# Attention over an adjacency matrix: groups of 4, 8, 8, 8, 4 row tiles instead of 4, 6, 8, 8, 6, and a rearranged start

## The chip, the cores and the metric

The kernel runs on one core of a Trainium2 chip. The metric is the device time of one launch in microseconds (us), of which three runs are given, and the profile is of one execution of its own. The core's engines are TensorE (PE, with its weight loads shown apart as PEld), VectorE (DVE), ScalarE (ACT), GpSimd (POOL) and SyncE (SP). Each works through its own instructions in the order in which they are written, and waits on semaphores for the others. Matrix products and transposes of TensorE land in PSUM, which here is divided into two double buffers for turned pairs, and one bank each for acc0, acc1, hist and misc.

## The reference, cut to what matters

```python
Wh, We = x @ W, entity_embs @ W                 # x, entity_embs: (4096, 64)
scores = (Wh @ a1)[:, None] + (We @ a2)[None, :]
e = where(scores > 0, scores, 0.2 * scores)     # leaky ReLU
e = where(adj > 0, e, -9e15)                    # adj: (4096, 4096) int32, 0 or 1
h = softmax(e, axis=1) @ entity_embs + x
out = layernorm(x + elu(h))
```

A score is p[i] + q[j], with one number p per row and one number q per entity, so the 4096 x 4096 matrix of scores is never made by a product. What is made for each of its places is a weight, the exponential of the masked score.

## The kernel before, in words

The 4096 rows are 32 tiles of 128. They are worked on in five groups of SIZES = (4, 6, 8, 8, 6) tiles. Within a group, the 4096 entities are 32 blocks of 128, and the work on one block of one group is a step; there are 160 steps. Two blocks make a pair, so a group has 16 pairs (GROUP_PAIRS), and the program has 80. Most instructions are issued once per step or per pair whatever the group's size; the size sets how wide they are: 512, 768 or 1024 columns for 4, 6 or 8 tiles.

What happens to a pair, in order:

- **Load.** POOL issues the adjacency as chunks of four blocks, which is two pairs (load(n), lines 282 to 292), converted to bf16 on the way. The ring raw holds RAWS = 5 chunks. Chunk n waits until the pairs of chunk n - 5 have been turned. Chunks 0 to 7 belong to group 0, 8 to 15 to group 1, 16 to 23 to group 2. Chunk 7 comes in two halves.
- **Turn.** TensorE transposes the pair into one of two PSUM buffers (turn_pair, L754). Pair j needs the mask of pair j - 2 made, since that frees its buffer.
- **Mask.** ACT (L340) or DVE (L553) writes it to SBUF, scaled. The function by_dve says which engine has which pair.
- **Histogram.** TensorE multiplies the mask with codes (add_hist, L770). After a group's 16 pairs the histogram is copied by ACT (copy_hist), spread by TensorE (spread_hist, L785), and decoded by DVE (decode, L518 to L537) into one bound per row, which keeps the exponentials in range. TensorE and ACT or DVE make a row of it (make_row, L792; take_row, L541 or L370).
- **Weigh.** For every pair DVE takes the minimum of mask and bound (masked, L564), and for every step it makes the exponent (exponents, L572), ACT takes the exponential (weights, L354), and TensorE multiplies it into acc0 (features, L805) and acc1 (sums, L808). The call is weigh(g, b); five buffers hold weights.
- **Finish.** While the next group is weighed, DVE, ACT and POOL finish the group in 11 parts placed at fixed steps (FINISH_AT): division, residual, elu, layer norm. The last group is finished by itself after its last step (finish_last).

Pairs are turned ahead of the steps that weigh them: 16 pairs before step 0, then all 16 pairs of group 1 during steps 0 to 19, and after that one pair for every two steps, 44 blocks ahead. So group 1 is turned while group 0 is weighed; group 2 is turned in steps 20 to 51, group 3 in steps 52 to 83, group 4 in steps 84 to 115, and the last 44 steps turn nothing.

The start, before step 0, has chains of its own. DVE makes q for all entities (q_columns). The highest and lowest q go through TensorE and back (q_highest L713, q_to_all L717, with DVE's q_scale in between); from them DVE makes the offsets from which ACT makes codes (L388). DVE then makes p (p_columns), its highest value goes through TensorE twice (p_highest, p_to_all), and find_shift makes the shift of the exponentials. The eight rows of p, spread over all partitions, are made by TensorE (p_row, L727) in the bank misc, and are copied by ACT (L328). DVE sums the entities (L679), 65 columns in one instruction, ahead of its first mask. All engines go through the 16 pairs of group 0 with these pieces written between the pairs.

Of the kernel before, what the change touches and what calls it, by code (L numbers as in the profile page):

```python
# [7 lines left out]
SIZES = (4, 6, 8, 8, 6)  # L8
# [44 lines left out]
ROWS_FROM = 8  # L53


def attention_layernorm(nc, x, adj, ent_blocks, turned_in, weights_in, out):
# [19 lines left out]
    with ctx:  # L76
# [173 lines left out]
        def by_dve(j):  # L250

            g, k = divmod(j, GROUP_PAIRS)
            return g == 0 and k >= 7 and k % 2 == 1 or g == 1 and k % 2 == 1 or g == 2 and k in (1, 4, 8, 12)
# [68 lines left out]
        def _(act):  # L322
# [3 lines left out]
            def p_row(c):  # L326
                act.wait_ge(p_mm, c + 1)
                act.activation(pb[:, 512 * c:512 * c + 512], misc[:, :], ACT.Copy, scale=1 - ALPHA).then_inc(p_rows, 1)  # L328
# [56 lines left out]
            for j in range(4):  # L385
                store_pair(j)
            act.wait_ge(offs_done, 2)
            act.activation(codes[:, :, :], offs, ACT.Exp, bias=code_bias[:, :], scale=SPAN * LN2).then_inc(codes_done, 1)  # L388
            for j in range(4, GROUP_PAIRS):
                if j >= ROWS_FROM:  # L390
                    p_row(j - ROWS_FROM)
                store_pair(j)
            copy_hist(0)
            act.wait_ge(bias_done, 1)
# [20 lines left out]
        def _(dve):  # L415
# [256 lines left out]

            q_columns()
# [5 lines left out]
            dve.tensor_reduce(ent_part[:, :], ent_sb[:, :, :].rearrange("p b f -> p f b"), AX.X, ALU.add).then_inc(part_done, 1)  # L679
            for j in range(GROUP_PAIRS):  # L680
                store_pair(j)
            decode(0)
            take_row(0)
            dve.wait_ge(p_rows, ROWS)
            masked(0)
            dve.wait_ge(sum_mm, 1)
            dve.tensor_copy(ent_sum[:, :], misc[:, 0:FA]).then_inc(sum_done, 1)
            for g in range(NG):
                for b in range(NB):
# [7 lines left out]
                    exponents(g, b)  # L697
                    if b % 2 == 0 and s + 2 < STEPS:
# [4 lines left out]
        def _(pe):  # L703
# [15 lines left out]
            def p_row(c):  # L719

                pe.wait_ge(pcol_step, 2)
                if c == 0:
                    pe.wait_ge(shift_step, 2)
                if c:
                    pe.wait_ge(p_rows, c)
                for t in range(4):
                    ins = pe.transpose(misc[:, P * t:P * t + P], pcol[:, 4 * c + t:4 * c + t + 1].to_broadcast([P, P]), identf[:, :])  # L727
# [10 lines left out]
            def entity_sums():  # L738
                pe.wait_ge(part_done, 1)
# [34 lines left out]
            def spread_hist(g):  # L774
                pe.wait_ge(hist_copied, g + 1)
                pe.wait_ge(stack_done, 2)
                if g == 0:
                    pe.wait_ge(shift_step, 3)
                    pe.wait_ge(p_rows, ROWS)
# [15 lines left out]
            def weigh(g, b):  # L795
                i = NB * g + b
                pe.wait_ge(w_done, i + 1)
                if b == 0 and g:
# [39 lines left out]
            q_highest()  # L838
            q_to_all()
# [69 lines left out]
```

## Time and profile before

| | us |
|---|---|
| median of 3 runs | 348.91 (348.24 to 349.12) |
| the profiled execution | 347.55 |
| its span | 345.5 |
| start, to the first exponent (step 0) | 48.8 |
| group 0 weighed, to step 32 | 48.8 to 94.4 |
| group 1 | 94.4 to 151.6 |
| group 2 | 151.6 to 216.5 |
| group 3 | 216.5 to 281.3 |
| group 4 | 281.3 to 330.9 |
| the last group's finish and output | 330.9 to 345.5 |

The borders are the starts of the first exponent (L572) of each group, and the end of the last one, in the timeline of DVE. In the rows below, a window row gives the window, its length, then for PE, PEld, DVE, ACT and POOL the busy time and the count of instructions, then TensorE's granted clock as a share of 2.4 GHz, the DMA engines' share and the GB/s that they wrote. A timeline row gives start, duration (or the time from the first start to the last end where several are merged), engine, line, operation, what is written from what, the count, and in brackets the idle time before it and what ended it.

Over the whole span the page has PE busy 295.0 us (85%), DVE 306.7 us (89%) and ACT 259.3 us (75%).

### The profile page before, as it was taken

The page shows a single profiled execution, that of the slowest core. Times are in us where ns is not written, and L with a number is a line of the kernel's source. Part 1 is how long each engine was busy: PE and PEld are TensorE (multiplying, and loading weights), DVE is VectorE, ACT ScalarE, POOL GpSimd, SP SyncE. Part 2 cuts the span into 40 slices and gives each one's busy share as a digit, 9 for nine tenths or more (in the row PEclk, how much of TensorE's full clock was granted, in tenths as well). Part 3 has the DMA queues.
Part 4 walks back from the last instruction along what each step waited for, and adds up shares of the span by engine and source line. Part 5 has one row for each costly group of instructions (what it writes and reads, how often), then busy time and mean ns, then how long its engine had stood idle before and what let it go on. Part 6 is the DMA issues. An engine that isn't in the chain of part 4 may idle for free.

```text
span 345.5 us, 9074 instructions
## 1 busy us (share of the span) xinstructions
PE 295.0 (85%) x3920; PEld 160.2 (46%) x3920; DVE 306.7 (89%) x428; ACT 259.3 (75%) x262; POOL 46.4 (13%) x55
## 2 busy tenths in 40 slices
PE   1285969999999999999999999999988598876860
PEld 1154756767755555654544445445443234422320
DVE  1797169899998998889999999999999999999965
ACT  1083729787998989999999998999886567565630
POOL 6031212222121111120000002100000400000301
PEclk9998969999999999999999999999999789999995
DMA  7999999999999999799667775700000000000000
GB/s 157 255 206 201 157 189 152 185 207 208 207 207 207 196 173 159 123 143 150 95 99 111 111 109 83 125 3 2 2 0 2 2 30 3 2 1 2 0 32 24
DMA packets 35768, 37.32 MB, mean 108 GB/s; under 512 B 848, under 2 KB 34960, under 8 KB 35728
## 3 DMA queue, kind: packets, MB, share of 16 engines
q0 software_dynamic: 33936, 33.56, 61.7%
q1 hardware_dynamic: 1792, 3.18, 3.2%
q8 instruction: 31, 0.51, 0.6%
q14 instruction: 9, 0.07, 0.1%
HBM read 69.24 MB, written 1.05 MB: 203 GB/s over the span
## 4 chain that ended last, share of the span: by engine, by line
PE 43%; DVE 23%; issue 22%; ACT 7%; DMA 2%; POOL 1%; POOLq 0%; DVEq 0%; SPq 0%; ACTq 0%
PE acc L805 15%; PE pairs L754 14%; DVE xm L564 10%; PE acc L808 8%; DVE wts L572 5%; ACT mask L340 4%; PE hist L770 3%; DMA ent_sb<-ent_blocks_dram 2%; ACT wts L354 2%; DVE y L606 1%; DVE ent_part L679 1%; POOL rstd L297 1%; PE misc L727 1%; PE misc L785 1%; DVE wts L431 1%
## 5 line engine op out<-in xcount | busy, mean ns | idle before, releaser
L354 ACT ACTIVATE wts<-wts,q_bias 128x768 f32<-128x768 f32 (+2 forms) x160 | 151.2, 977 | 41.1 <-DVE wts L572 40.8
L572 DVE SCALAR_TENSOR_TENSOR wts<-pb,q_bend,xm 128x768 f32<-128x768 f32 (+2 forms) x160 | 166.3, 1063 | 2.5 <-PE acc L808 2.2
L805 PE MATMUL acc<-wts,ent_sb 128*32 128x384 f32 (+2 forms) x1280 | 151.2, 520 | 10.8 <-ACT wts L354 8.5
L340 ACT ACTIVATE mask<-pairs 128x2048 bf16<-128x2048 bf16 (+2 forms) x64 | 98.9, 1548 | 23.3 <-PE pairs L754 22.5
L808 PE MATMUL acc<-wts,onesf 128*32 128x256 f32 (+1 forms) x1152 | 91.8, 359 | 0.0
L564 DVE TENSOR_TENSOR xm<-mask,drow 128x1536 bf16<-128x1536 bf16 (+2 forms) x80 | 80.2, 1003 | 0.1
L754 PE MATMUL pairs<-ident,raw 128*128 128x128 bf16 x1024 | 75.4, 228 | 4.3 <-DVE mask L553 3.2
L754 PEld LDWEIGHTS pairs<-ident,raw 128*128 128x128 bf16 x1024 | 62.5, 102 | 26.4 <-issue 26.1
L808 PEld LDWEIGHTS acc<-wts,onesf 128*32 128x32 f32 x1152 | 40.8, 111 | 71.2 <-issue 65.5
L288 POOL DMA_DIRECT2D raw<-adj_dram x40 | 33.3, 834 | 179.0 <-PE pairs L754 178.2
L805 PEld LDWEIGHTS acc<-wts,ent_sb 128*32 128x32 f32 x1280 | 36.7, 109 | 36.6 <-ACT wts L354 17.7
L770 PE MATMUL hist<-mask,codes 128*32 128x384 bf16 (+2 forms) x320 | 33.3, 349 | 2.4 <-ACT mask L340 1.4
L297 POOL TENSOR_TENSOR rstd<-var,mhalf 128x6 f32<-128x6 f32 (+2 forms) x5 | 11.0, 2205 | 116.6 <-DVE var L643 116.6
L553 DVE TENSOR_SCALAR mask<-pairs 128x1536 bf16<-128x1536 bf16 (+3 forms) x17 | 15.7, 925 | 11.8 <-PE pairs L754 11.7
L770 PEld LDWEIGHTS hist<-mask,codes 128*32 128x32 bf16 x320 | 9.9, 96 | 9.6 <-ACT mask L340 2.2
L328 ACT ACTIVATE pb<-misc 128x512 f32<-128x512 f32 x8 | 4.8, 598 | 8.0 <-PE misc L727 8.0
L713 PE MATMUL misc<-identf,qm 128*2 128x128 f32 x2 | 0.6, 398 | 9.8 <-DVE qm L439 9.8
L792 PE MATMUL misc<-ident,dcol 128*128 128x128 bf16 x32 | 3.2, 248 | 5.5 <-DVE dcol L536 5.5
L606 DVE SCALAR_TENSOR_TENSOR y<-ent_sum,empty,misc 128x64 f32<-128x64 f32 x32 | 6.6, 273 | 0.0
L727 PE MATMUL misc<-identf,pcol 128*128 128x128 f32 x32 | 5.5, 298 | 0.9 <-DVE shift L500 0.2
L647 DVE TENSOR_TENSOR y<-y,rstd 128x384 f32<-128x384 f32 (+2 forms) x5 | 2.9, 581 | 3.8 <-POOL rstd L297 3.6
L431 DVE TENSOR_TENSOR wts<-ent_sb,wa_row 128x2048 f32<-128x2048 f32 x1 | 2.3, 2293 | 4.2 <-DMA ent_sb<-ent_blocks_dram 4.2
(107 smaller groups left out, 103.0 us busy)
## 6 DMA issues: line engine op xcount, KB each, us to landing
raw<-adj_dram POOLq DMA_DIRECT2D x16, 1024.0 KB, 12.6
raw<-adj_dram POOLq DMA_DIRECT2D x16, 768.0 KB, 8.0
raw<-adj_dram POOLq DMA_DIRECT2D x7, 512.0 KB, 12.1
ent_sb<-ent_blocks_dram SPq DMA_DIRECT2D x1, 1024.0 KB, 7.8
x_sb<-x_dram SPq DMA_DIRECT2D x2, 256.0 KB, 8.1
raw<-adj_dram POOLq DMA_DIRECT2D x2, 256.0 KB, 5.7
out_dram<-y SPq DMA_DIRECT2D x2, 256.0 KB, 2.0
x_sb<-x_dram SPq DMA_DIRECT2D x2, 192.0 KB, 8.0
```

Of the source, the lines that this page charges most:

```text
L288: pool.dma_start(raw[:, n % RAWS, 0:SIZES[g], 0:P * first], rows(adj, g)[:, :, P * CHUNK * c:P * (CHUNK * c + first)]).then_inc(adj_in[n % ...
L297: pool.tensor_tensor(rstd[:, 0:n], var[:, 0:n], mhalf[:, 0:n], ALU.pow).then_inc(rstd_done, 1)
L340: act.activation(mask[:, i % RING:i % RING + k, 0:n], pairs[j % 2][:, 0:k, 0:n], ACT.Relu, scale=2.0 ** LIFT).then_inc(act_mask_done, 1)
L354: act.activation(part, part, ACT.Exp, bias=q_bias[:, b:b + 1]).then_inc(w_done, 1)
L553: dve.tensor_scalar(mask[:, i % RING + k:i % RING + 2, 0:n], pairs[j % 2][:, k:2, 0:n], 2.0 ** LIFT, 0.0, ALU.mult, ALU.max).then_inc(dve_ ...
L564: dve.tensor_tensor(xm[:, i % XS:i % XS + 2, 0:n], mask[:, i % RING:i % RING + 2, 0:n], drow[:, g % 2, 0:n].unsqueeze(1).to_broadcast([P, ...
L572: dve.scalar_tensor_tensor(wts[:, i % SLOTS, 0:n], pb[:, P * TILE0[g]:P * TILE0[g] + n], q_bend[:, b:b + 1], xm[:, i % XS, 0:n], ALU.max, ...
L606: ins = dve.scalar_tensor_tensor(y[:, t, :], ent_sum[:, 0:F], empty[:, row:row + 1], misc[:, features_at(g, t)], ALU.mult, ALU.add)
L754: ins = pe.transpose(pairs[j % 2][:, k, P * t:P * t + P], raw[:, n % RAWS, t, at:at + P], ident[:, :])
L770: ins = pe.matmul(hist[to:to + Q, 0:n], codes[:, i % NB, :], mask[:, i % RING, n * c:n * c + n], start=(pair == 0), stop=(pair == GROUP_PA ...
L805: pe.matmul(acc[0][to:to + Q, 0:n], ent_sb[:, b, Q * f:Q * f + Q], part[:, n * k:n * k + n], start=(b == 0), stop=(b == NB - 1))
L808: ins = pe.matmul(acc[1][Q * k:Q * k + Q, 0:P * m], onesf[:, 0:Q], part[:, P * t:P * t + P * m], start=(b == 0), stop=(b == NB - 1))
```

## The change

The diff has five parts. SIZES becomes (4, 8, 8, 8, 4). TensorE turns pairs 0 to 3 before it does q_highest and q_to_all, and ACT makes codes before pair 7 and not before pair 4; the histogram's products start at pair 10, in threes. Rows of p are made in acc0 and acc1 in turn instead of misc; row 0 goes between pairs 13 and 14, the others come after the last pair. DVE's sum of the entities is cut in two halves of 32 and 33 columns, behind its masks of pairs 13 and 15, and of group 0 DVE makes these masks alone (before: pairs 7, 9, 11, 13 and half of 15). The sums of the entities are copied at step 2 and no more ahead of step 0.

```diff
-SIZES = (4, 6, 8, 8, 6)
+SIZES = (4, 8, 8, 8, 4)
...
-            return g == 0 and k >= 7 and k % 2 == 1 or g == 1 and k % 2 == 1 or g == 2 and k in (1, 4, 8, 12)
+            return g == 0 and k in (13, 15) or g == 1 and k % 2 == 1 or g == 2 and k in (1, 4, 8, 12)
...
-            for j in range(4):
-                store_pair(j)
-            act.wait_ge(offs_done, 2)
-            act.activation(codes[:, :, :], offs, ACT.Exp, bias=code_bias[:, :], scale=SPAN * LN2).then_inc(codes_done, 1)
-            for j in range(4, GROUP_PAIRS):
-                if j >= ROWS_FROM:
-                    p_row(j - ROWS_FROM)
-                store_pair(j)
+            for j in range(GROUP_PAIRS):
+                store_pair(j)
+                if j == CODES_AT:
+                    act.wait_ge(offs_done, 2)
+                    act.activation(codes[:, :, :], offs, ACT.Exp, bias=code_bias[:, :], scale=SPAN * LN2).then_inc(codes_done, 1)
+                if j == GROUP_PAIRS - 2:
+                    p_row(0)
             copy_hist(0)
+            for c in range(1, ROWS):
+                p_row(c)
...
-            dve.tensor_reduce(ent_part[:, :], ent_sb[:, :, :].rearrange("p b f -> p f b"), AX.X, ALU.add).then_inc(part_done, 1)
             for j in range(GROUP_PAIRS):
                 store_pair(j)
+                if by_dve(j):
+                    entity_part(j // (GROUP_PAIRS - 1))
             decode(0)
             take_row(0)
-            dve.wait_ge(p_rows, ROWS)
             masked(0)
-            dve.wait_ge(sum_mm, 1)
-            dve.tensor_copy(ent_sum[:, :], misc[:, 0:FA]).then_inc(sum_done, 1)
+            dve.wait_ge(p_rows, 1)
...
+                    if s == 2:
+                        dve.wait_ge(p_rows, ROWS)
+                        dve.wait_ge(sum_mm, 1)
+                        dve.tensor_copy(ent_sum[:, :], misc[:, 0:FA]).then_inc(sum_done, 1)
...
             def weigh(g, b):
                 i = NB * g + b
                 pe.wait_ge(w_done, i + 1)
+                if i == 0:
+                    pe.wait_ge(p_rows, ROWS)
...
-            q_highest()
-            q_to_all()
-            pe.wait_ge(ident_done, 4)
...
+            pe.wait_ge(ident_done, 4)
             for j in range(GROUP_PAIRS):
-                if j >= ROWS_FROM:
-                    p_row(j - ROWS_FROM)
                 turn_pair(j)
-                if j == 6:
+                if j == 3:
+                    q_highest()
+                    q_to_all()
+                if j == 12:
                     p_highest()
-                if j == 7:
+                if j == 13:
                     p_to_all()
-                if j >= 4:
-                    hist_to(j - 1)
+                    p_row(0)
+                hist_to(min(j - 1, 3 * (j - 9)))
             hist_to(GROUP_PAIRS)
+            p_row(1)
             spread_hist(0)
+            for c in range(2, 5):
+                p_row(c)
             make_row(0)
+            for c in range(5, ROWS):
+                p_row(c)
             entity_sums()
```

CODES_AT is 7, tested after store_pair(7): codes are made behind the mask of pair 7. On TensorE the program began like this before (misc<-identf,qm is the exchange's first product, pairs<-ident,raw are turns, eight per pair of group 0, hist<-mask,codes the histogram):

```order
L707 MATMUL acc<-w_sb,wts 128x64 x2
L713 MATMUL misc<-identf,qm 2x128
L717 MATMUL misc<-q_diag,onesf 128x2
L754 MATMUL pairs<-ident,raw 128x128 x40
L770 MATMUL hist<-mask,codes 32x256 x12
L754 MATMUL pairs<-ident,raw 128x128 x8
L770 MATMUL hist<-mask,codes 32x256 x4
```

Now it begins like this, still on TensorE:

```order
L716 MATMUL acc<-w_sb,wts 128x64 x2
L761 MATMUL pairs<-ident,raw 128x128 x32
L722 MATMUL misc<-identf,qm 2x128
L726 MATMUL misc<-q_diag,onesf 128x2
L761 MATMUL pairs<-ident,raw 128x128 x56
L777 MATMUL hist<-mask,codes 32x256 x12
L761 MATMUL pairs<-ident,raw 128x128 x8
```

The 32 turns of pairs 0 to 3 moved ahead of the exchange, and eleven pairs are turned before the first product with codes instead of five.

Where TensorE passes from the start to the first steps, the program before has these rows (misc<-stack spreads the histogram, misc<-ident,dcol is make_row, misc<-ent_part the sums of the entities, acc<-wts the first weigh):

```order
L770 MATMUL hist<-mask,codes 32x256 x12
L785 MATMUL misc<-stack,acc_sb 128x64 x2
L792 MATMUL misc<-ident,dcol 128x128 x4
L741 MATMUL misc<-ent_part,onesf 128x65
L754 MATMUL pairs<-ident,raw 128x128 x24
L805 MATMUL acc<-wts,ent_sb 32x256 x4
```

After the change TensorE has these in the same place (acc<-identf,pcol are rows of p, four transposes each):

```order
L734 MATMUL acc<-identf,pcol 128x128 x4
L791 MATMUL misc<-stack,acc_sb 128x64 x2
L734 MATMUL acc<-identf,pcol 128x128 x12
L798 MATMUL misc<-ident,dcol 128x128 x4
L734 MATMUL acc<-identf,pcol 128x128 x12
L748 MATMUL misc<-ent_part,onesf 128x65
L761 MATMUL pairs<-ident,raw 128x128 x32
L813 MATMUL acc<-wts,ent_sb 32x256 x4
```

Seven rows of p moved from between the pairs to around the decoding, and the first two pairs of group 1 have 32 transposes instead of 24.

## Rows read from the trace of the kernel before

**Rows 1.** Busy time of each engine by window, one per stage (columns above)
```profile
48.80:94.40 45.60, 45.17 (x832) 31.91 (x830) 42.74 (x66) 37.69 (x44) 8.60 (x10) 0.96 1.20 192
76.20:94.40 18.20, 18.20 (x351) 13.02 (x350) 16.93 (x29) 15.61 (x18) 2.64 (x3) 1.00 1.24 208
94.40:151.60 57.20, 56.69 (x793) 32.40 (x790) 52.50 (x74) 53.75 (x52) 8.05 (x9) 1.00 1.08 175
151.60:216.50 64.90, 64.83 (x851) 32.83 (x849) 63.82 (x74) 62.99 (x55) 8.35 (x9) 1.00 0.73 112
216.50:281.30 64.80, 58.56 (x704) 25.80 (x706) 64.59 (x76) 52.86 (x50) 4.63 (x2) 0.95 0.11 20
281.30:330.90 49.60, 40.42 (x476) 16.03 (x468) 49.53 (x67) 31.65 (x36) 3.21 (x1) 1.00 0.02 7
330.90:345.50 14.60, 3.35 (x35) 1.69 (x35) 7.21 (x20) 2.00 (x4) 1.32 (x1) 0.68 0.04 14
```

**Rows 2.** Timeline of TensorE in the start
```profile
14.44 0.59 PE L713 MATMUL misc<-identf,qm 128*2 128x128 f32 x2 [9.77 <-DVE qm L439]
...
32.66 1.01 PE L754 MATMUL pairs<-ident,raw 128*128 128x128 bf16 x8 [3.22 <-DVE mask L553]
...
48.40 1.91 PE L754 MATMUL pairs<-ident,raw 128*128 128x128 bf16 x16
```

**Rows 3.** Timeline of DVE in the start
```profile
28.06 3.85 DVE L679 TENSOR_REDUCE ent_part<-ent_sb 128x65 f32<-128x2080 f32 x1
```

**Rows 4.** DMA issues from 3 to 4 us: chunk 1, size, us to landing
```profile
raw<-adj_dram POOLq DMA_DIRECT2D x1, 512.0 KB, 12.1
```

**Rows 5.** Timeline of POOL: chunks 1 to 4 are issued
```profile
3.55 2.98 POOL L288 DMA_DIRECT2D raw<-adj_dram  x4
```

**Rows 6.** The tile mask, 10 to 50 us: count, duration ns min/median/max, first and last start
```profile
L340 ACT ACTIVATE mask<-pairs x12: 597/1018/1025, 17.2 to 42.9; 128x1024 bf16<-128x1024 bf16 x11, 128x512 bf16<-128x512 bf16 x1
```

**Rows 7.** Timeline of TensorE in groups 0 (turning 6 tiles) and 1 (turning 8)
```profile
62.06 0.84 PE L754 MATMUL pairs<-ident,raw 128*128 128x128 bf16 x12
62.83 0.35 PE L770 MATMUL hist<-mask,codes 128*32 128x384 bf16 x4
...
118.75 1.07 PE L754 MATMUL pairs<-ident,raw 128*128 128x128 bf16 x16
...
120.84 0.39 PE L770 MATMUL hist<-mask,codes 128*32 128x512 bf16 x3
...
122.25 1.07 PE L754 MATMUL pairs<-ident,raw 128*128 128x128 bf16 x16
```

**Rows 8.** Chain of waits in order of time: start, us, what
```profile
79.61 1.00 PE pairs L754 x16
...
167.90 1.00 PE pairs L754 x16
171.84 1.00 PE pairs L754 x16
```

**Rows 9.** Timeline of DVE: exponents of 4 tiles and of 6
```profile
88.23 1.41 DVE L572 SCALAR_TENSOR_TENSOR wts<-pb,q_bend,xm 128x512 f32<-128x512 f32 x2
...
90.16 1.41 DVE L572 SCALAR_TENSOR_TENSOR wts<-pb,q_bend,xm 128x512 f32<-128x512 f32 x2
...
283.07 1.94 DVE L572 SCALAR_TENSOR_TENSOR wts<-pb,q_bend,xm 128x768 f32<-128x768 f32 x2
...
285.80 1.94 DVE L572 SCALAR_TENSOR_TENSOR wts<-pb,q_bend,xm 128x768 f32<-128x768 f32 x2
```

**Rows 10.** Line L621, one part of the finish, duration ns min/median/max
```profile
L621 DVE TENSOR_TENSOR y<-y,total x5: 419/559/684, 116.1 to 336.2; 128x384 f32<-128x384 f32 x2, 128x512 f32<-128x512 f32 x2, 128x256 f32<-128x256 f32 x1
```

**Rows 11.** Timeline of TensorE around the decoding in group 3
```profile
267.48 1.04 PE L805 MATMUL acc<-wts,ent_sb 128*32 128x512 f32 x8
...
272.76 0.82 PE L792 MATMUL misc<-ident,dcol 128*128 128x128 bf16 x6 [3.81 <-DVE dcol L536]
273.51 1.94 PE L805 MATMUL acc<-wts,ent_sb 128*32 128x512 f32 x8
```

More of the change, by code:

```diff
@@ L52 @@
 ROWS = N // 512
-ROWS_FROM = 8
+CODES_AT = 7
 def attention_layernorm(nc, x, adj, ent_blocks, turned_in, weights_in, out):
@@ L327, in p_row @@
                 act.wait_ge(p_mm, c + 1)
-                act.activation(pb[:, 512 * c:512 * c + 512], misc[:, :], ACT.Copy, scale=1 - ALPHA).then_inc(p_rows, 1)
+                act.activation(pb[:, 512 * c:512 * c + 512], acc[c % 2][:, :], ACT.Copy, scale=1 - ALPHA).then_inc(p_rows, 1)
             def store_pair(j):
@@ L671, in finish_last, with entity_part @@
                     finish(g, part)
+            def entity_part(k):
+                f = slice(0, Q) if k == 0 else slice(Q, FA)
+                dve.tensor_reduce(ent_part[:, f], ent_sb[:, :, f].rearrange("p b f -> p f b"), AX.X, ALU.add).then_inc(part_done, 1)
             q_columns()
@@ L721, in p_row @@
                 pe.wait_ge(pcol_step, 2)
[L722 to L725, printed above, removed]
+                if c >= 2:
+                    pe.wait_ge(p_rows, c - 1)
                 for t in range(4):
-                    ins = pe.transpose(misc[:, P * t:P * t + P], pcol[:, 4 * c + t:4 * c + t + 1].to_broadcast([P, P]), identf[:, :])
+                    ins = pe.transpose(acc[c % 2][:, P * t:P * t + P], pcol[:, 4 * c + t:4 * c + t + 1].to_broadcast([P, P]), identf[:, :])
                 ins.then_inc(p_mm, 1)
@@ L738, in entity_sums @@
             def entity_sums():
-                pe.wait_ge(part_done, 1)
+                pe.wait_ge(part_done, 2)
                 pe.wait_ge(drow_done, 1)
@@ L778, in spread_hist @@
                     pe.wait_ge(shift_step, 3)
-                    pe.wait_ge(p_rows, ROWS)
                 if g == 1:
```

## The prediction, made before the changed kernel ran

> **What bounds the kernel now.** I read the windows by stage first, then the timelines of the start, then the chain of waits. In group 0 TensorE is busy 45.17 of 45.6 us, and in group 1 56.69 of 57.2, while DVE has 52.50 and ACT 53.75 there [rows 1]: TensorE bounds both. In group 2 all three are full (64.83, 63.82 and 62.99 of 64.9). In group 3 DVE has 64.59 of 64.8, in group 4 49.53 of 49.6: DVE alone bounds them, and TensorE has room (40.42). The first 48.8 us are dependency chains: TensorE starts the exchange for q at 14.44 and waits 3.22 us at 32.66 for a mask of DVE [rows 2], which stood behind DVE's sum of the entities, 3.85 us from 28.06 [rows 3]. The end is a serial finish, 14.6 us.
>
> **Group 4 gets narrower.** DVE makes two exponents and one minimum per two steps. With 4 tiles that takes 90.16 - 88.23 = 1.93 us, with 6 tiles 285.80 - 283.07 = 2.73 [rows 9]. So 16 times 0.80 = 12.8 us go. One minimum of the group, and its decoding, are made in group 3: 12.5 go in group 4, and 0.3 and an estimate of 0.1 in group 3. TensorE, at 40.42 of 49.6 us [rows 1], loses about a third of its columns there and stays within DVE's 37.1. The part of the finish of group 3 that lies in it stays. **-12.9.**
>
> **The last finish gets narrower.** One of its DVE operations takes 0.56 us with 6 tiles and 0.42 with 4 (the median and the least) [rows 10]. Nine such in a row give 9 x 0.14 = 1.3; I add an estimate of 1.4 for six additions of features that become four (0.2 us each: 0.4), GpSimd's power, the last exponential, the last product and the copies, at a third of each. Bounds 1.8 and 3.4. **-2.7.**
>
> **Group 1 gets wider.** On TensorE, two steps with one turned pair take 122.25 - 118.75 = 3.50 us when 6 tiles are weighed [rows 7], and 171.84 - 167.90 = 3.94 when 8 are [rows 8]. For 16 pairs that is +7.0, so 57.2 becomes 64.2. On DVE the step from 6 to 8 tiles costs what that from 4 to 6 cost, +12.8, so 52.50 becomes 65.3 busy. DVE becomes the bound. With about 0.5 of idle as in group 2 (64.9 elapsed, 63.82 busy, two thirds of 1.1) the group takes 65.9. Bounds: 64.2 (TensorE alone), and 68 if the idle of DVE in the old group 1, 4.7, stays by more than half. **+8.7.**
>
> **Group 2 finishes a wider group.** Finishing group 1 beside it costs DVE eight operations of 0.684 instead of 0.559 [rows 10], 1.0, and two more additions of features, 0.4. DVE was at 63.82 of 64.9, so most is paid. The narrower turns of group 4 take load from TensorE and ACT only. Bounds 0.4 and 1.8. **+1.1.**
>
> **The start.** Turning pair 0 needs chunk 0 only, and pairs 2 and 3 chunk 1. Chunk 1 is issued at 3.6 [rows 5] and lands after 12.1 us [rows 4], at 15.7. TensorE takes its instructions in order, so the exchange, ready at 14.44 [rows 2], now stands behind the turns of pairs 2 and 3, about 1 us each as at 32.66: it begins at 17.8, 3.4 us late, and all of DVE's work on q, codes and p with it. Against that, four pairs are masked by then, and the wait at 32.66 goes. From there ACT sets the pace: masks of 1.02 us [rows 6]. I go through them: masks of pairs 4 to 7 end at about 25.0, codes at 26.1, pairs 8 to 12 at about 32.2, pair 14 at 35.8, the half of pair 15 at 37.0. Then come the histogram's copy and DVE's second half of the sum (1.95 us, from 37.0), the decoding until 40.5 (an estimate of 1.6 for seven short operations), the row (0.6), DVE's copy and the minimum, and the first exponent at about 42.5 instead of 48.8. Adjacency data permit it: at 208 GB/s [rows 1] 512 KiB take 2.5 us, so chunk 7 lands at about 15.7 + 6 x 2.5 = 31. The seven rows of p behind the last pair cost ACT 0.6 us each, as 512 columns of a mask do (the least) [rows 6], and go beside DVE's decoding; TensorE's first product now waits for all of them, at about 43.3. TensorE turns its first pair of group 1 at 43.6 instead of 48.40 [rows 2], hence **-4.7** for TensorE, which is what counts, since it bounds group 0; bounds -2 and -6.5. The entity sums' copy moved to step 2 waits for nothing that is later than 43.4, so it costs nothing; without that cover it would cost up to 1 us.
>
> **Group 0 turns wider pairs.** A pair's turns take 1.07 instead of 0.84 us, and its histogram 0.39 instead of 0.35 [rows 7]: 16 x 0.27 = 4.3. The first pairs run at half clock, as 16 transposes in 1.91 us at 48.40 [rows 2] show, +0.5; a spread product and two row transposes more, +0.4. All of it is on the bounding engine: **+5.2.** GpSimd issues the same number of loads, eight of them a third larger. Eight chunks of 1 MiB at 208 GB/s take 40 us; from 31 they land by 71.5, and chunk 16, needed for the first turn of group 2, by 76.5. That turn stood at 79.61 [rows 8], and would stand at 79.6 - 4.7 + 4.8 = 79.7. So the loads just hide, with 3 us to spare, and a start that gained more than that would have it taken back.
>
> **The sum:** -4.7 + 5.2 + 8.7 + 1.1 - 0.4 - 12.5 - 2.7 = -5.3 us, the terms in the order group 0's start and turns, groups 1, 2, 3, 4, the end. The span goes from 345.5 to 340.2, the profiled execution from 347.55 to about 342.3. The median of the runs, 348.91, is 1.4 above that execution; taken against it the forecast is 343.6, and I say 343.8, as the loss in group 1 has more room above than below. A difference under 0.3%, 1.05 us, could not be told from none.
>
> **The rivals.**
>
> *The start's gain is lost to loads or to the exchange* (12%). If chunks land at 190 GB/s, or the exchange is later than 17.8 because the loads of x and of the entities share the engines with chunk 1, group 0 ends 2 to 3 us later. For it: 192 GB/s stood in the whole of group 0; against it: 208 in its second half [rows 1], where loads were queued. It gives -5.3 + 2.7 = -2.6, 346.3.
>
> *TensorE has slack in group 0* (14%). If the 0.43 us of idle in the row understates, since busy time of matmuls is modelled, the start's 6.3 us come through whole and a part of the 5.2 is hidden: -9, 339.9. For it: ACT is at 37.69 and DVE at 42.74 of 45.6, far enough to let TensorE catch up; against it, turns follow products without a gap in the rows.
>
> *Three full engines get in each other's way in group 1* (9%), the one that ends on the other side. Group 1 would have DVE at 65.3, TensorE at 64.2 and ACT near the 62.99 of group 2; two PSUM buffers for turned pairs couple them, and the two masks that DVE makes in the group stand behind exponents. If a step there takes 2.25 us and not 2.06, as if each pair waited 0.4 us more, the group takes 72, +6, and the result is 349.8. It is slower than before from 2.23 us a step on. Against it: group 2 ran at 64.9 / 32 = 2.03 with the same three loads.
>
> *TensorE's clock falls in group 4* (4%). In group 3 TensorE idled 3.81 us at 272.76, and the next weigh had 1.94 us where 1.04 stood before [rows 11]: half clock, 1.2 GHz. If all of group 4 ran so, weighing 4 tiles would take TensorE an estimated 1.3 us a step (half of the 1.94 for the features, and 0.3 for the sums), and DVE's 0.97 (1.93 / 2) would wait: 32 x 0.33, +10. For half of the group it is +5, 348.8. Against it: TensorE is busy about three quarters of a step in the new group 4, as in the old one, whose clock was 1.00 [rows 1].
> The Trainium skill (TensorE: Matmul & The Clock Gate, Part 1: The HAM clock gate) says that "the default state is throttled, and activity releases the throttle". The row at 272.76 agrees; by that rule a group in which TensorE has less to do would be the one to fear.
>
> **How the numbers follow.** The forecast has 61%, with its own range 341.3 to 346.5 from the bounds of its terms. The range of all, 340.8 to 348.0, leaves out about 2 in 10, at the ends of the second and the last two rivals. Faster by over 0.3%: 61 + 12 + 14 - 1 = 86%; within 0.3%: most of the clock's 4 and a third of the third rival's 9, 7%; slower 7%.
>
> **What would show it.** Exchange at 17.8; first exponent at 42.5; the first turn of group 2 near 79.7 with no wait for a load; group 0's end at 94.4 - 4.7 + 5.2 = 94.9; group 1 in 65.9 with DVE over 98% busy; group 2 in 66.0; group 3 in 64.4; group 4 in 37.1 at clock 1.00; the end in 11.9. I am wrong if TensorE waits for raw in group 0, if group 1 exceeds 70, or if group 4 exceeds 40 with TensorE full.

## The result, and the profile after

The changed kernel takes 339.86 us, the median of 4 runs (339.81 to 339.96), against 348.58 us for the kernel before in 4 runs (347.85 to 349.12). The ratio is 0.975, with a 95% interval of 0.973 to 0.977: 8.7 us faster. The forecast was 5.1 us, so the direction was right, and the time came out 0.9 us below the low end of the range. The profiled execution took 339.86 us, its span 337.8. All times here and below are of executions in the faster of the chip's two states, but for the profiled execution of sizes_only, which was a slow one (365.13 us, clock 0.833), so that kernel's stages can't be read.

The windows of the changed kernel by stage, with the columns of [rows 1], from the first exponent on:

```profile
42.10:93.40 51.30, 49.06 (x907) 35.35 (x907) 45.58 (x66) 42.16 (x46) 8.74 (x10) 1.00 1.24 208
93.40:158.00 64.60, 63.47 (x855) 32.70 (x853) 64.39 (x73) 59.49 (x52) 8.74 (x9) 1.00 1.07 175
158.00:225.10 67.10, 64.61 (x836) 31.60 (x837) 65.32 (x76) 62.38 (x56) 8.61 (x10) 1.00 0.53 80
225.10:289.40 64.30, 56.10 (x671) 23.04 (x664) 64.09 (x76) 48.00 (x49) 3.87 (x2) 0.95 0.08 14
289.40:326.50 37.10, 27.07 (x524) 14.74 (x512) 37.02 (x67) 24.44 (x36) 2.67 (x1) 1.00 0.02 7
326.50:337.80 11.30, 2.18 (x36) 1.26 (x36) 5.40 (x17) 1.55 (x4) 1.01 (x1) 0.73 0.06 21
```

Beside [rows 1] and beside the forecast, in us:

| stage | before | forecast | after |
|---|---|---|---|
| start, to the first exponent | 48.8 | 42.5 | 42.1 |
| group 0 | 45.6 | to 94.9 | 51.3, to 93.4 |
| group 1 | 57.2 | 65.9 | 64.6 |
| group 2 | 64.9 | 66.0 | 67.1 |
| group 3 | 64.8 | 64.4 | 64.3 |
| group 4 | 49.6 | 37.1 | 37.1 |
| the end | 14.6 | 11.9 | 11.3 |
| span | 345.5 | 340.2 | 337.8 |

TensorE's timeline of the changed kernel in the start and at the first turn of group 2 (to be read against [rows 2]):

```profile
15.90 1.89 PE L761 MATMUL pairs<-ident,raw 128*128 128x128 bf16 x16 [3.17 <-DMA raw<-adj_dram]
17.72 0.58 PE L722 MATMUL misc<-identf,qm 128*2 128x128 f32 x2
...
28.47 1.03 PE L761 MATMUL pairs<-ident,raw 128*128 128x128 bf16 x8
...
31.90 0.62 PE L761 MATMUL pairs<-ident,raw 128*128 128x128 bf16 x8
...
37.00 0.29 PE L777 MATMUL hist<-mask,codes 128*32 128x256 bf16 x4 [1.20 <-DVE mask L554]
...
42.61 1.95 PE L761 MATMUL pairs<-ident,raw 128*128 128x128 bf16 x32
...
73.07 1.07 PE L761 MATMUL pairs<-ident,raw 128*128 128x128 bf16 x16 [0.42 <-DMA raw<-adj_dram]
...
78.11 1.07 PE L761 MATMUL pairs<-ident,raw 128*128 128x128 bf16 x16 [0.34 <-DMA raw<-adj_dram]
```

The exchange for q begins at 17.72 behind the turns of pairs 2 and 3, 3.3 us later than before. The wait of 3.22 us for a mask [rows 2] is down to 1.20. A turn of eight transposes takes 1.03 us at 28.47 and 0.62 at 31.90: in between, at 31.4, the granted clock went from 1.2 to 2.4 GHz. The first turns of group 1 (32 transposes in 1.95 us) are made at 2.4 where those of before (24 in 2.77) were made at 1.2. They begin at 42.61, 5.8 us earlier than before. At 73.07 and 78.11 TensorE waits for loads, chunks 15 and 16; the turn at 78.11 is the first of group 2.

DVE in the start of the changed kernel, with the two halves of the sum (one piece of 3.85 us before, [rows 3]) and the first exponent:

```profile
34.54 1.98 DVE L677 TENSOR_REDUCE ent_part<-ent_sb 128x32 f32<-128x1024 f32 x1
...
36.77 2.04 DVE L677 TENSOR_REDUCE ent_part<-ent_sb 128x33 f32<-128x1056 f32 x1
...
42.14 0.75 DVE L573 SCALAR_TENSOR_TENSOR wts<-pb,q_bend,xm 128x512 f32<-128x512 f32 x1
```

And the chain of waits of the changed kernel across group 0:

```profile
57.26 1.01 PE pairs L761 x16
58.55 19.51 DMA raw<-adj_dram
78.11 1.07 PE pairs L761 x16
```

This chunk 16 lands at 78.06, and its turn starts at 78.11. No such row stands in group 0 of the kernel before, where chunk 16 landed at 75.2 and its turn began at 79.5.

### The profile page after: what moved, and what is told of

Read it like the earlier page. It is cut to its first block, busy times and chain, and to the rows that moved or that the text cites. A ratio compares the mean times of both kernels' runs of the same rounds, so it can differ in the third digit from the quotient of the medians.

```text
span 337.8 us, 9328 instructions
## 1 busy us (share of the span) xinstructions
PE 287.4 (85%) x4046; PEld 157.6 (47%) x4046; DVE 305.8 (91%) x426; ACT 258.7 (77%) x265; POOL 46.2 (14%) x55
## 4 chain that ended last, share of the span: by engine, by line
PE 28%; DVE 26%; issue 24%; DMA 9%; ACT 9%; POOL 1%; POOLq 0%; DVEq 0%; ACTq 0%
DVE xm L565 13%; PE acc L813 10%; PE pairs L761 10%; DMA raw<-adj_dram 9%; DVE wts L573 7%; ACT mask L340 5%; PE acc L816 5%; ACT wts L354 3%; PE hist L777 2%; DVE ent_part L677 1%; DVE y L607 1%; POOL rstd L297 1%; DVE var L641 1%; DVE y L632 1%; DVE above L522 0%
## 5 line engine op out<-in xcount | busy, mean ns | idle before, releaser
L354 ACT ACTIVATE wts<-wts,q_bias 128x1024 f32<-128x1024 f32 (+1 forms) x160 | 151.9, 977 | 41.7 <-DVE wts L573 41.3
L573 DVE SCALAR_TENSOR_TENSOR wts<-pb,q_bend,xm 128x1024 f32<-128x1024 f32 (+1 forms) x160 | 166.4, 1064 | 2.5 <-PE acc L816 2.3
L813 PE MATMUL acc<-wts,ent_sb 128*32 128x512 f32 (+1 forms) x1280 | 143.1, 520 | 14.1 <-ACT wts L354 9.3
L816 PE MATMUL acc<-wts,onesf 128*32 128x256 f32 (+1 forms) x1280 | 85.3, 339 | 0.0
L565 DVE TENSOR_TENSOR xm<-mask,drow 128x2048 bf16<-128x2048 bf16 (+1 forms) x80 | 80.4, 1004 | 0.1
L813 PEld LDWEIGHTS acc<-wts,ent_sb 128*32 128x32 f32 x1280 | 32.6, 110 | 36.7 <-ACT wts L354 20.1
L777 PE MATMUL hist<-mask,codes 128*32 128x512 bf16 (+1 forms) x320 | 27.8, 353 | 3.4 <-ACT mask L340 2.2
L297 POOL TENSOR_TENSOR rstd<-var,mhalf 128x8 f32<-128x8 f32 (+1 forms) x5 | 11.0, 2196 | 102.6 <-DVE var L644 102.5
L554 DVE TENSOR_SCALAR mask<-pairs 128x2048 bf16<-128x2048 bf16 (+2 forms) x14 | 15.8, 1127 | 4.9 <-PE pairs L761 4.9
L328 ACT ACTIVATE pb<-acc 128x512 f32<-128x512 f32 x8 | 4.6, 596 | 1.6 <-PE acc L734 1.6
L734 PE MATMUL acc<-identf,pcol 128*128 128x128 f32 x32 | 4.7, 278 | 0.6 <-ACT pb L328 0.6
```

Of the source, the lines that this page charges most:

```text
L297: pool.tensor_tensor(rstd[:, 0:n], var[:, 0:n], mhalf[:, 0:n], ALU.pow).then_inc(rstd_done, 1)
L354: act.activation(part, part, ACT.Exp, bias=q_bias[:, b:b + 1]).then_inc(w_done, 1)
L554: dve.tensor_scalar(mask[:, i % RING + k:i % RING + 2, 0:n], pairs[j % 2][:, k:2, 0:n], 2.0 ** LIFT, 0.0, ALU.mult, ALU.max).then_inc(dve_ ...
L565: dve.tensor_tensor(xm[:, i % XS:i % XS + 2, 0:n], mask[:, i % RING:i % RING + 2, 0:n], drow[:, g % 2, 0:n].unsqueeze(1).to_broadcast([P, ...
L573: dve.scalar_tensor_tensor(wts[:, i % SLOTS, 0:n], pb[:, P * TILE0[g]:P * TILE0[g] + n], q_bend[:, b:b + 1], xm[:, i % XS, 0:n], ALU.max, ...
L777: ins = pe.matmul(hist[to:to + Q, 0:n], codes[:, i % NB, :], mask[:, i % RING, n * c:n * c + n], start=(pair == 0), stop=(pair == GROUP_PA ...
```

## Experiments

All are compared with the kernel before, run on the same chip as the experiment (its medians there lie between 348.08 and 348.32); the ratios have 95% intervals. "After" is the changed kernel. The letters of the theories in the expectations are theirs.

### The two halves of the change by themselves

sizes_only is the kernel before with the new group sizes:

```diff
-SIZES = (4, 6, 8, 8, 6)
+SIZES = (4, 8, 8, 8, 4)
```

> The kernel before with the sizes 4, 8, 8, 8, 4 and nothing else. Theory A (group 0 of the changed kernel is bound by the loads, which run without a break at 208 GB/s, so that start and sizes compete there): alone, the sizes start from the old start and are not held by loads; group 0 then ends near 99, group 1 takes 64.6, group 2 67.1, group 3 64.3, group 4 37.1, the end 11.3: span about 343.5, 2 us less than before. Rival B (the sizes alone gave most of the 7.7 us of span): below 341.

346.37 us, the median of 11 runs (346.05 to 347.02), ratio 0.995 (0.994 to 0.997): by the ratio about 1.6 us faster, near the 2 of theory A; B is out.

start_only is the changed kernel with the old sizes, the same line turned round.

> The changed kernel with the old sizes 4, 6, 8, 8, 6. Theory A: TensorE starts to turn group 1 at 42.6 instead of 48.4 and at full clock; chunks of 768 KiB leave the loads 4 us of room, so the whole 7 us come through: group 0 ends at 87.4, the rest as before, span about 338.5. If A holds, the two parts sum to -9 and the whole gives -7.7. Rival B: the start gives no more than the 5 us that were predicted for TensorE, span 340.5 or more, with group 0 ending at 90.

339.67 us (339.11 to 341.65), ratio 0.976 (0.973 to 0.979). The new start alone brings 8.5 us, as much as the whole change. Its groups and its end last as long as before, 45.6, 57.2, 64.9, 64.8, 49.6 and 14.6 us, and the first exponent comes at 40.4, 8.4 us earlier: a span of 337.1, where theory A had 338.5 and rival B 340.5 or more. So the two halves don't add: -8.5 and -1.6 alone, -8.7 together. On top of the new start the new sizes are worth nothing that can be measured.

### Do the loads bind?

load_after gives the changed kernel 1 MiB of extra transfers beside chunks 9 and 13, into tiles that are not in use yet; load_start has the same edit and the old sizes:

```diff
+                if n in (9, 13):
+                    for i, a in enumerate((y, e)):
...
+                        pool.dma_start(spare, rows(adj, 0)[:, 0:2, P * CHUNK * i:P * CHUNK * (i + 1)]).then_inc(spare_in[i], 16)
```

> The changed kernel with 1 MiB more of loads in group 0's time (four of 256 KiB into tiles not in use yet, two before chunk 9 and two before chunk 13). Theory A: the loads bind the first turn of group 2, so 5.0 us of transfers more, less 0 to 1 us of room, come out: group 0 ends 4 to 5 us later, and about the same on the span, since groups 1 to 3 are full. Rival (TensorE binds group 0, the 0.8 us of waits for raw are chance): under 1.5 us.

> The same 1 MiB more of loads in the kernel with the new start and the old sizes. Theory A: the loads have 4 us of room at the first turn of group 2 there, so of 5.0 us 0 to 1.5 come out. Rival: as much as in the changed kernel.

load_after took 345.44 us (344.75 to 345.80), 5.6 more than after; load_start 341.08 (340.92 to 341.47), 1.4 more than start_only. Group 0 grew from 51.3 to 56.6 in the first and from 45.6 to 45.9 in the second. The waits in the window 42 to 100, first of load_after, then of load_start (engine, tile and line, waited for; total, times, longest):

```profile
PEld pairs L771 <- DMA raw<-adj_dram: 5.7, 5, 3.9
PE pairs L771 <- DMA raw<-adj_dram: 4.3, 3, 3.6
```
```profile
PEld pairs L771 <- DMA raw<-adj_dram: 0.5, 1, 0.5
PE pairs L771 <- DMA raw<-adj_dram: 0.2, 1, 0.2
```

1 MiB takes 5.1 us at 208 GB/s, and with the new sizes all of it reaches the time: group 0 is 5.3 us longer, where theory A had 4 to 5 (TensorE's clock was at half from 69.3 to 72.7 there, which may be in it). The loads have no room left there: in the changed kernel chunks 9 to 19 landed 4.8 to 5.1 us apart, without a break from 42.7 to 93.3. With the old sizes nearly all is hidden. The rest of load_start's loss is its start: of the 2.1 us between the spans, 1.8 lie ahead of the first exponent, at 42.2 and not 40.4 (see the clock, below).

light_loads makes the chunks of group 1 three quarters as large, and turns tile 5 in place of tiles 6 and 7, so two tiles of that group are computed from wrong rows; the count of turns stays.

```diff
-                pool.dma_start(raw[:, n % RAWS, 0:SIZES[g], 0:P * first],
+                m = 6 if g == 1 else SIZES[g]
+                pool.dma_start(raw[:, n % RAWS, 0:m, 0:P * first],
...
-                        ins = pe.transpose(pairs[j % 2][:, k, P * t:P * t + P], raw[:, n % RAWS, t, at:at + P], ident[:, :])
+                        ins = pe.transpose(pairs[j % 2][:, k, P * t:P * t + P], raw[:, n % RAWS, min(t, 5) if i // NB == 1 else t, at:at + P], ident[:, :])
```

> The changed kernel with chunks of group 1 that load 6 of its 8 tiles; tiles 7 and 8 are turned from the data of tile 6, so TensorE, ACT and DVE do the same work on a quarter less of loads in group 0, and two tiles of group 1 are computed from the wrong rows. Theory A' (loads alone hold group 0 in the changed kernel): the 5.7 us that group 0 grew by fall to what TensorE's wider turns cost, forecast 4.3 to 5.2, and the runs spread by 1 to 3 us again, as in the new start with old sizes; total 338 to 339.5. Rival F (wider turns hardly cost, the loads are all of it): group 0 back to 47 or less, total 335 to 336.5.

339.59 us (337.66 to 340.34), ratio 0.974 (0.972 to 0.976). Its first exponent was at 42.4, and the turn of pair 32, which no load held (chunk 16 had landed at 68.9), at 77.46:

```profile
77.46 1.07 PE L762 MATMUL pairs<-ident,raw 128*128 128x128 bf16 x16
```

Group 0 took 50.4 us and not 51.3. Of the 5.7 us by which it grew, 0.9 are the loads', and 4.8 stay when they are gone, within the 4.3 to 5.2 of theory A'; rival F is out. Of the 4.8, 0.4 come ahead of the third pair turned in the group, where TensorE waits for ACT's first mask (1.86 us long and not 1.43; on this wait see the clock, below), and 4.3 from there on, where the chain of waits runs through TensorE's wider turns and products.

That the loads cap group 0 shows in another run too: in masks_g3 (below) the first exponent came 0.7 us later than in the changed kernel, at 42.83, and group 0 ended at 93.45 all the same, against 93.42. By light_loads a start like start_only's, with its exponent at 40.4, would end group 0 near 90.8 (an estimate, 40.4 + 50.4) if no load held it; with the loads as they are that gain is lost. That is why the halves don't add: without the loads' 0.9 the stages of the new sizes give 4.8 + 7.4 + 2.2 - 0.5 - 12.5 - 3.3 = -1.9, near the -1.6 of sizes_only, whose late start leaves the loads more time. The cap may also be why the changed kernel's four runs lie within 0.15 us, while those here spread over 2.7 and those of start_only over 2.5. That isn't shown: after_warm (below) spreads over 1.4 with the same loads.

### The pieces of the start

start_exchange1 and start_exchange0 have the old sizes, with the exchange for q behind pair 1 and ahead of pair 0 (the diff is the first's):

```diff
-                if j == 3:
+                if j == 1:
                     q_highest()
                     q_to_all()
```

> The new start with the old sizes, and the exchange for q between pairs 1 and 2 instead of behind pair 3: it begins at 14.6 instead of 17.7. Theory C (ACT's masks and the arrival of the chunks set the pace of the start, the exchange being 3.4 us late costs nothing): codes are made at the same time, since they stand behind the mask of pair 7; first exponent within 0.5 us, total within 1 us of the new start with old sizes (339.7). Rival D (the late exchange costs what it is late, through p and the shift): 2 to 3 us faster, 337.

> The new start with the old sizes, and the exchange ahead of all turns, as in the kernel before. Theory C: pairs 0 and 1 are turned at 16.2 and not at 10.9, ACT has 2 masks, 2 us, less done when chunk 1 is there, and the first exponent comes 1.5 to 2 us later than in the new start: total 341 to 342. Rival D: faster than the new start, since q and p are 3.4 us earlier.

340.00 us (339.22 to 341.21) and 342.45 (339.80 to 342.81), against 339.67 with the exchange behind pair 3. In start_exchange1 it began at 14.74, about as before, and the first exponent came no sooner for that, at 42.15. TensorE's clock was at half from 26.4 to 29.8 and from 36.6 to 40.0 there, so the two exponents don't compare cleanly, but the fastest runs, 339.2 and 339.1, agree too. A gain of the 2 to 3 us of rival D is out: the late exchange costs nothing that these runs show, as masks are made meanwhile. With the exchange first, two runs took 339.8 and four 342.4 to 342.8, so it is at best no better (the profiled one of these took 342.48, with its first exponent at 43.7).

start_one_sum has the old sizes, and DVE sums the entities in one piece behind its mask of pair 13:

```diff
-                f = slice(0, Q) if k == 0 else slice(Q, FA)
-                dve.tensor_reduce(ent_part[:, f], ent_sb[:, :, f].rearrange("p b f -> p f b"), AX.X, ALU.add).then_inc(part_done, 1)
+                if k == 0:
+                    dve.tensor_reduce(ent_part[:, :], ent_sb[:, :, :].rearrange("p b f -> p f b"), AX.X, ALU.add).then_inc(part_done, 2)
```

> The new start with the old sizes, and the sum of the entities in one instruction of 3.9 us behind the mask of pair 13. DVE's half of pair 15 waits for it, about 38.4 instead of 36.4, but no second half follows before the decoding: histogram, spread and decoding come 1 to 1.5 us later, decoding itself starts at about 39.5 instead of 38.7. First exponent 0.8 to 1.5 us later, total +1. Rival (the halves bring nothing): within 0.5 us.

343.86 us (342.54 to 344.25), ratio 0.987 (0.984 to 0.990): 4.2 more than start_only, where about 1 was expected. Its timeline, DVE and then TensorE:

```profile
32.81 3.87 DVE L677 TENSOR_REDUCE ent_part<-ent_sb 128x65 f32<-128x2080 f32 x1
...
37.16 0.41 PE L777 MATMUL hist<-mask,codes 128*32 128x256 bf16 x4 [3.08 <-DVE mask L554]
37.50 1.12 PE L734 MATMUL acc<-identf,pcol 128*128 128x128 f32 x4
```

The half mask of pair 15 stands behind the sum, and TensorE idles 3.08 us ahead of the last histogram products instead of the 1.20 of after and of start_only. Four transposes of row 1 of p then take 1.12 us, where the changed kernel has 0.65 at 37.22; the granted clock was at half from 35.4 to 42.2. The first exponent comes at 43.8. Of the 4.2 us, then, 3.4 are seen in the profile: the last histogram products come 1.9 us later than in start_only (35.24), and 1.5 more are lost from there to the exponent, in the stretch at half clock. The idle and the clock weren't tried apart.

### TensorE's clock

before_warm is the kernel before with 16 transposes that nothing reads, in the gaps around the decoding:

```diff
             spread_hist(0)
+            for _ in range(10):
+                pe.transpose(acc[0][:, 0:P], identf[:, :], identf[:, :])
             make_row(0)
+            for _ in range(6):
+                pe.transpose(acc[0][:, 0:P], identf[:, :], identf[:, :])
```

> The kernel before, with 16 transposes more on TensorE in its two idle gaps around the decoding of group 0, into a bank that is overwritten later. Theory E (rows of p moved into these gaps keep TensorE's clock up, and that is part of the gain): the granted clock stays 1.00 from 46 to 53 us where it was 0.5, the first turns of group 1 take half as long, and the total falls by 1 to 2 us. Rival (the clock at the start falls elsewhere or costs nothing): within 0.5 us.

```profile
45.77 1.26 PE L861 MATMUL acc<-identf 128*128 128x128 f32 x10
...
48.87 1.50 PE L754 MATMUL pairs<-ident,raw 128*128 128x128 bf16 x24
```

The first two pairs of group 1 are turned in 1.50 us instead of 2.77, at 2.4 GHz, and the clock is full from 38.7 on. They end at 50.4 and not 51.2, though the first exponent comes later, at 49.4 and not 48.8. Yet group 0 still takes 45.6 us and the kernel 348.15 (346.97 to 349.06, 12 runs; ratio 1.000, 0.998 to 1.002): theory E is out. The first turns aren't what group 0 waits for. The third pair turned in it is, pair 18, here in the kernel before and in before_warm:

```profile
53.03 0.83 PE L754 MATMUL pairs<-ident,raw 128*128 128x128 bf16 x12 [0.43 <-ACT mask L340]
```
```profile
53.60 0.83 PE L754 MATMUL pairs<-ident,raw 128*128 128x128 bf16 x12 [1.77 <-ACT mask L340]
```

TensorE waits there for ACT's mask of pair 16, which frees the buffer, and in ACT's program that mask stands behind the weights of steps 0 and 1, so behind the first exponents. The chain of waits of the kernel before runs just so:

```profile
48.78 0.74 DVE wts L572
49.52 0.60 DVE xm L564
50.12 0.68 DVE wts L572
50.82 0.72 ACT wts L354
51.55 1.35 ACT mask L340
53.03 0.83 PE pairs L754 x12
```

In all eight kernels profiled with the old sizes the turn of pair 18 starts 4.2 to 4.3 us behind the first exponent, whether the turns ahead of it ended 1.0 us (before_warm) or 2.4 us (before) behind it; and in seven of them, with first exponents from 40.4 to 49.4, group 0 lasted 45.6 (in load_start, with its added transfers, 45.9). So the first exponent is the border that counts, and what it gains counts in full unless loads hold the group.

start_warm puts 48 such transposes into start_only, and after_warm into the changed kernel:

```diff
+            keep_busy(24)
             for j in range(GROUP_PAIRS):
                 turn_pair(j)
+                if j == 1:
+                    keep_busy(16)
...
+            hist_to(GROUP_PAIRS - 1)
+            keep_busy(8)
```

> The new start with the old sizes, and 48 transposes of the identity more on TensorE in its idle times of the start: 24 ahead of the first turn, 16 where it waits for chunk 1, 8 where it waits for the last mask. Theory J (what differs between executions, and between the profiles with the first exponent at 40.4 and at 42.1, is TensorE at half clock for a stretch between 26 and 42 us, and idle time before that lets the clock fall): the clock is full over the start, first exponent at 40.4 or earlier in every execution, total 339.2 or less, and the runs lie within 1 us instead of 2.5. Rival (the half clock falls into the start whatever TensorE does): 339.7, spread as before.

> The same 48 transposes in the changed kernel. Theory A with J: the first exponent comes up to 1.7 us earlier, at 40.4, but the first turn of group 2 stays at 78.1, when its chunk lands, group 0 gets longer by what the start got shorter, and the total stays within 0.5 us of 339.86. Rival (loads do not cap it): 338.5 or less.

start_warm took 340.42 us (340.08 to 341.59) and after_warm 340.93 (340.14 to 341.51), 0.75 and 1.1 more than without. The first difference is not clear of the runs' spread; the second is, as all six runs lie above the changed kernel's four. Neither the gain that theory J forecast nor, in after_warm, a total within 0.5 us came. TensorE's timeline of start_warm, and its window from 20 to 30:

```profile
4.60 4.83 PE L855 MATMUL acc<-identf 128*128 128x128 f32 x24
10.81 1.07 PE L761 MATMUL pairs<-ident,raw 128*128 128x128 bf16 x16 [1.38 <-DMA raw<-adj_dram]
...
21.25 1.89 PE L761 MATMUL pairs<-ident,raw 128*128 128x128 bf16 x16 [0.83 <-DMA raw<-adj_dram]
```
```profile
20.00:30.00 10.00, 7.84 (x79) 5.75 (x78) 7.21 (x11) 8.24 (x9) 4.14 (x5) 0.50 1.28 205
```

The clock was full early, from 8.7: pairs 0 and 1 were turned in 1.07 us. At 19.0 it fell to half, and stayed there until 32.6, while TensorE turned pairs in bursts with short waits for loads. In start_only the clock rose at 25.1, during the same turns, and in the changed kernel at 31.4 (the step from 1.03 to 0.62 us above). Here is start_only at the time at which the changed kernel still has 1.03:

```profile
27.50 0.62 PE L761 MATMUL pairs<-ident,raw 128*128 128x128 bf16 x8
```

The eight transposes of one and the same pair start at 26.52 in start_only and 26.77 in the changed kernel, and those of a pair three turns on at 30.13 and 31.90: with turns and products at half clock in between, the later one has all of the 1.8 us between the first exponents at 40.4 and 42.1. Why the clock rises in one execution at 25.1 and in another at 31.4 stays open; this filler did not have it stay up.

In after_warm the clock fell likewise (full from 9.8 to 16.6, half to 30.3), the first exponent came at 41.92, 0.2 us sooner than without filler, and chunk 16 landed at 78.7 and not 78.1; group 0 took 52.1. Its span is 1.6 us longer than the changed kernel's: 0.6 are there at the end of group 0, and 0.9 come in groups 2 and 3; the cause of the latter stays open.

### Groups 1 and 2

masks_g2 takes two of DVE's four masks in group 2's pairs away, and ACT makes them; masks_g3 leaves those and gives DVE two of group 3's:

```diff
-            return g == 0 and k in (13, 15) or g == 1 and k % 2 == 1 or g == 2 and k in (1, 4, 8, 12)
+            return g == 0 and k in (13, 15) or g == 1 and k % 2 == 1 or g == 2 and k in (1, 4)
```
```diff
-            return g == 0 and k in (13, 15) or g == 1 and k % 2 == 1 or g == 2 and k in (1, 4, 8, 12)
+            return g == 0 and k in (13, 15) or g == 1 and k % 2 == 1 or g == 2 and k in (1, 4, 8, 12) or g == 3 and k in (7, 11)
```

> The changed kernel, with DVE's two masks of group 2 that fall into group 1 (pairs 8 and 12) made by ACT. Theory G (TensorE binds group 1, one pair in 3.93 us from pair 40 to 49, DVE only fills up): group 1 takes 64 or more, total within 0.7 us of 339.9. Rival H, the term as I predicted it (DVE binds group 1): 2.3 us less of DVE, group 1 takes 63.0 or less, total 1.3 us or more faster.

> The changed kernel, with two masks of group 3 (pairs 7 and 11, made in group 2's first 20 steps) made by DVE and not by ACT. Theory I (ACT, busy 41.7 of 42.0 us in these steps, binds them): 3.6 us less of ACT against 2.3 more of DVE, group 2 takes 66 or less instead of 67.1, total 0.7 to 1.3 us faster. Rival (DVE or TensorE bind them): the same or up to 1.5 us slower.

339.61 us (339.19 to 339.89) and 342.08 (341.28 to 342.63), against 339.86. The window of group 1 in masks_g2 (with 1.0 us beside the group, so that it is as long as after's), and that of group 2 in masks_g3 (without its last 0.8 us):

```profile
92.60:157.20 64.60, 63.66 (x868) 32.97 (x860) 63.30 (x73) 64.11 (x56) 8.10 (x9) 1.00 1.07 175
```
```profile
158.00:226.00 68.00, 64.45 (x812) 31.21 (x814) 66.83 (x77) 59.39 (x54) 9.07 (x9) 0.97 0.52 79
```

Group 2's pairs are turned during group 1, so masks_g2 takes DVE work from group 1: 63.30 busy where after has 64.39. The group shrinks by 1.0, to 63.6, and the end grows by 0.6; the total gains 0.25, which is not told from none. The group lies between the 64 of theory G and the 63.0 of rival H. TensorE's pairs are what is left: with fewer masks for DVE pair 49 is still turned at 140.2, as in the changed kernel, and in both most turns from pair 40 on come 3.93 us apart:

```profile
120.58 1.07 PE L761 MATMUL pairs<-ident,raw 128*128 128x128 bf16 x16
...
124.51 1.07 PE L761 MATMUL pairs<-ident,raw 128*128 128x128 bf16 x16
```

16 x 3.93 = 62.9. In masks_g3 two masks more for DVE and two fewer for ACT make group 2 1.6 us longer (68.7), and DVE is busy 66.83 us in 68.0 of it where it was 65.32 in 67.1. So ACT doesn't set that group, as theory I had it, and DVE's added work is in the time. Half clock from 218.6 to 222.0, the 0.97 of the row, may have a part in it. Of the 2.2 us that masks_g3 is slower, another 0.4 are in its end.

## Why the prediction was too small, step by step

**The start and group 0: forecast +0.5 on the border, measured -1.0.** The walk through the start held up to the first exponent: exchange forecast 17.8, measured 17.72; first exponent 42.5 and 42.14. What failed was the step behind it, that TensorE's first turn of group 1 "is what counts, since it bounds group 0": it priced the start at -4.7 where the first exponent gave -6.3 (the walk's own 43.6 against 48.40 is -4.8). The first turn was also put too late: it came at 42.61, a gain of 5.8, as it stands ahead of the first product and does not wait for ACT's copy of the last row of p. But the exponent's gain, measured 6.64, is what counts, in full: before_warm shows that the first turns can be 1.3 us faster for nothing, start_only turns an exponent 8.4 us earlier into 8.4 us of span, and pair 18's turn shows why (the mask that it waits for). For the same reason the +0.5 for the first pairs at half clock had no place in the sum; nor were they at half clock. The group's growth was forecast 5.2 and is 5.66: 4.75 by light_loads, of which 4.3 are on TensorE (4.3 and 0.4 were counted there) and 0.4 in ACT's first mask, and 0.9 for loads. -6.64 + 5.66 is the measured -1.0.

**The loads.** I left 3 us to spare at chunk 16, with its landing at 76.5 and its turn at 79.7. Both are 78.1. The landing came later since the last half of chunk 7 landed at 32.6 and not at 31; the turn would have come near 77.2 by light_loads (35.1 behind the first exponent). The margin was below nothing. The last chunk of group 0 was the term that was off: 1.6 us of the miss at chunk 16 were there already at chunk 7. My warning that a larger gain of the start "would have it taken back" holds, only that 0.9 us were taken back already at the gain that was made; load_after and masks_g3 show the cap.

**Group 1: +8.7 forecast, +7.4 measured.** DVE's busy time was overestimated at 65.3; it is 64.39. The low bound, TensorE's own 64.2, was nearly the time, 64.6. masks_g2 gets below it, so it wasn't quite a bound, and the two masks on DVE are worth about 1 us of the group.

**Group 2: +1.1 forecast, +2.2 measured.** DVE is busy 65.32 against 63.82: +1.5, near the 1.4 that I counted. The rest is idle, of which these are a part, the waits of DVE for the sums' product of TensorE in the first 42 us of the group, after and then before:

```profile
DVE wts L573 <- PE acc L816: 1.6, 3, 0.7
```
```profile
DVE wts L572 <- PE acc L808: 0.8, 2, 0.4
```

By masks_g3 ACT doesn't set the group and more work on DVE lengthens it. The 0.7 wasn't tried apart.

**Groups 3 and 4 and the end: -15.6 forecast, -16.3 measured** (-0.5, -12.5 and -3.3). Group 4's 37.1 came out exactly, at clock 1.00; the end lost 0.6 more than I took, within its bounds.

**From the span to the median.** The forecast carried over that the median lay 1.4 us above the profiled execution, and added 0.2. That was chance of one execution: runs of the kernel before lie between 346 and 349.5. The changed kernel's median is its profiled execution's time.

In spans the miss is 2.4 us (forecast -5.3, measured -7.7): 1.5 + 1.3 - 1.1 + 0.1 + 0.6. The other 1.5 of the miss of 3.9 in time is that carry-over. Of the rivals, *TensorE has slack in group 0* named the time that was measured (339.9), by luck as to the number. Half its mechanism came: TensorE did have slack, the 0.43 us ahead of pair 18, and the start came through whole; but nothing of the wider turns was hidden. *The start's gain is lost to loads or to the exchange* was right on the place, at 0.9 us. Three engines in each other's way and a falling clock in group 4 didn't occur.

## What to carry to other kernels

Give a start its price where the steady state begins to run at its own pace (here the first exponent), and test it by shifting only that border, as seven profiles with a 45.6 us group did here. A busy share near 100% in a stage (45.17 of 45.6 us) doesn't say that its first instruction is the border; follow the chain of waits to where the stage's first wait ends. When a change makes transfers larger, list the landings against the turns with the measured rate from the last landing on, before trusting a margin of 3 us. Measure the parts of a joint change alone: here one part had the whole gain, and the other, on top of it, merely moved 15.8 us out of group 4 and the end into earlier groups.

## What was not expected of the hardware

- In a start full of short waits, full clock once reached didn't last: in start_warm it was full from 8.7 to 19.0 and half from 19.0 to 32.6, though TensorE worked more before that than in start_only (11.7 us of the first 20, against 6.7). The Trainium skill (TensorE: Matmul & The Clock Gate, Part 1: The HAM clock gate) has activity release the throttle. The 1.07 us for 16 transposes at 10.81, behind 24 filler transposes, agrees. The 1.89 at 21.25 shows it back at half, in a stretch (20 to 30) in which TensorE was busy 7.84 of 10 us.
- Ahead of its first recorded change the granted clock of a window reads 1.00 here also where it is at half: of start_only and the changed kernel alike the row says 1.00 for 20 to 30 us, where eight transposes take 0.62 us in one and 1.03 in the other. There the durations must be read.
- The converting loads ran at one steady rate: 208 GB/s written in all of group 0 of the changed kernel, a chunk of 1 MiB every 5.1 us, and in start_only chunks of 768 KiB every 3.8 to 3.9 us (chunks 8 to 12).
